# Selective-scan network on one core: GpSimd forms the scan inputs of layer 0 two states at a time

## The reference, cut to what matters

```python
dts, Bsx, Csx = jnp.split(x_dbl, [R, R + N], axis=2)
delta = jax.nn.softplus(dts + dt_projs_bias[None, :, :, None])
A = -jnp.exp(A_logs).reshape(K, DI, N)
def step(h, inp):
    ul, dl, bl, cl = inp
    dA = jnp.exp(dl[..., None] * A)
    h = dA * h + (dl * ul)[..., None] * bl[:, :, None, :]
    y = jnp.einsum('bkdn,bkn->bkd', h, cl)
    return (h, y)
```

## Time and profile before

| | |
|---|---|
| median of 3 runs | 18,193.1 us (18,173.5 to 18,209.19) |
| profiled execution | 18,181.2 us, its span 18,179.3 us |
| VectorE busy | 15,465.9 us, 85% |
| GpSimd busy | 14,606.0 us, 80% |
| TensorE busy | 13,277.9 us, 73% |
| ScalarE busy | 9,704.7 us, 53% |
| DMA | 2348 MB, mean 129 GB/s |

### The profile page before, as it was taken

The page is one execution under the profiler, slowest core; times in us unless marked ns, Lnnn a source line. Parts: engine busy times, 40 slices in busy tenths (PEclk is TensorE's granted clock), DMA queues, the critical chain, the costliest instruction groups (busy, mean ns, idle before and its releaser), DMA issues.

```text
span 18179.3 us, 131102 instructions
## 1 busy us (share of the span) xinstructions
PE 13277.9 (73%) x29696; PEld 5276.7 (29%) x29696; DVE 15465.9 (85%) x9374; ACT 9704.7 (53%) x9235; POOL 14606.0 (80%) x6213
## 2 busy tenths in 40 slices
PE   6776767767677686776767767677676776777767
PEld 2222322223222232222322223222232222322223
DVE  8888878888888888888888888888888888888888
ACT  4445744457444574445744456444564445644456
POOL 7996779967789677996778967799677996779967
PEclk9998989989899898998989989899898998989989
DMA  4442244422444224442244422444224442244422
GB/s 153 165 166 87 74 152 165 166 88 74 153 165 166 87 74 154 166 166 86 74 156 163 166 88 74 155 163 166 87 74 155 164 166 87 74 155 163 166 86 74
DMA packets 662527, 2348.03 MB, mean 129 GB/s; under 512 B 75452, under 2 KB 97224, under 8 KB 661704
## 3 DMA queue, kind: packets, MB, share of 16 engines
q1 hardware_dynamic: 661704, 2339.01, 37.3%
HBM read 2322.98 MB, written 15.73 MB: 129 GB/s over the span
## 4 chain that ended last, share of the span: by engine, by line
POOL 29%; PE 25%; issue 23%; DVE 12%; DMA 5%; ACT 4%; POOLq 1%; DVEq 0%; SPq 0%; ACTq 0%
POOL room L829 20%; PE bank L474 11%; DMA room<-bc_rows 5%; DVE room L1087 4%; PE bank L354 4%; PE bank L483 3%; POOL room L838 3%; PE bank L398 2%; DVE room L1107 2%; PE bank L508 2%; DVE room L1008 2%; PE bank L426 2%; POOL room L787 2%; POOL room L812 1%; DVE room L1016 1%
## 5 line engine op out<-in xcount | busy, mean ns | idle before, releaser
L1008 DVE TENSOR_TENSOR_SCAN room<-bank,room 128x1024 f32<-128x1024 f32 x3072 | 6964.6, 2279 | 530.9 <-ACT bank L613 428.1
L829 POOL TENSOR_TENSOR room<-room 128x1024 f32<-128x1024 f32 x3072 | 7177.0, 2364 | 190.9 <-DMA room<-bc_rows 128.2
L426 PE MATMUL bank<-room,identity 128*128 128x512 f32 x12288 | 6367.3, 646 | 267.3 <-DVE y L1027 252.6
L613 ACT ACTIVATE bank<-room,a 128x1024 f32<-128x1024 f32 x3072 | 3401.6, 1115 | 4910.0 <-DVE room L1008 4906.4
L474 PE MATMUL bank<-room,identity 128*128 128x512 f32 x6144 | 3135.3, 658 | 1231.9 <-DVE room L1107 908.2
L1087 DVE TENSOR_TENSOR_SCAN room<-bank,room 128x1024 f32<-128x1024 f32 x1536 | 3438.9, 2273 | 19.9 <-POOL room L884 4.0
L1016 DVE TENSOR_TENSOR room<-room,bank 128x1024 f32<-128x1024 f32 x2544 | 3044.3, 1197 | 368.7 <-PE bank L413 367.1
L426 PEld LDWEIGHTS bank<-room,identity 128*128 128x128 f32 x12288 | 2468.7, 204 | 2892.1 <-issue 2187.1
L413 PE MATMUL bank<-parts,pick_row 96*128 96x512 bf16 x5088 | 1602.9, 397 | 2333.7 <-DVE room L1016 2264.0
L884 POOL TENSOR_TENSOR room<-room 128x1024 f32<-128x1024 f32 x768 | 2330.9, 3058 | 63.2 <-POOL room L876 63.2
L474 PEld LDWEIGHTS bank<-room,identity 128*128 128x128 f32 x6144 | 1257.2, 210 | 3048.8 <-issue 2672.9
(11 more groups left out here) (98 smaller groups left out, 11593.6 us busy)
## 6 DMA issues: line engine op xcount, KB each, us to landing
room<-bc_rows SPq DMA_DIRECT2D x4368, 512.0 KB, 4.3
wx<-in_w_x SPq DMA_DIRECT2D x65, 162.0 KB
bc_rows<-xdbl SPq DMA_DIRECT2D x72, 128.0 KB, 2.0
xT<-in_x SPq DMA_DIRECT2D x8, 768.0 KB, 5.6
out_x<-xT SPq DMA_DIRECT2D x8, 768.0 KB, 4.4
win<-in_w_in SPq DMA_DIRECT2D x16, 288.0 KB, 3.2
room<-in_w_in SPq DMA_DIRECT2D x16, 288.0 KB, 4.0
room<-in_w_out SPq DMA_DIRECT2D x16, 288.0 KB, 4.3
```

What stands on the lines that cost most here:

```text
L426: ins = nc.tensor.matmul(bank[:, YACC + h, :], identity[:, :], state0[:, g % STATES, halves(h)], start=(n == 0), stop=(n == N - 1))
L613: nc.scalar.activation(whole(DECAY0[g % 2]), delta0[:, j, :], ACT.Exp, scale=a0[:, col:col + 1]).then_inc(S["decay"], note("decay", (i, j, ...
L829: nc.gpsimd.tensor_tensor(source0[:, g % SOURCES, :], du0[:, j, :], b_ring0[:, g % BROWS, :], ALU.mult).then_inc(S["source"], note("source ...
L1008: nc.vector.tensor_tensor_scan(run(state0[:, g % STATES, :]), run(whole(DECAY0[g % 2])), run(source0[:, g % SOURCES, :]), 0.0, ALU.mult, A ...
```

## The change

Two neighbouring units, n even and n + 1, share one instruction on GpSimd and one DMA on SyncE. The source instruction reads `du0[j]` twice (a broadcast over the pair), two neighbouring slots of the B ring, and writes two neighbouring slots of `source0`. It adds 2 to the semaphore `source`, and the scans of both units wait for that. SyncE fills two slots with one DMA of 1 MB, once the pair of sources two pairs before is made. SOURCES goes from 5 to 6 and STATES from 8 to 7, in the same memory. The rows of C, all other operations and their places in GpSimd's list by unit stay as they are.

```diff
--- before.py
+++ after.py
@@ -25,7 +25,9 @@
 
 UNITS = [(i, j, n) for i in range(K) for j in range(J) for n in range(N)]
 PASSES = K * J
-SOURCES, STATES, BROWS, CROWS = 5, 8, 4, 3
+SOURCES, STATES, BROWS, CROWS = 6, 7, 4, 3
+
+PAIR = 2
 
 POOL_LAG, SUM_LAG = 3, 4
 
@@ -149,7 +151,7 @@
 
 
         delta0, du0 = room[:, 0:3, :], room[:, 3:6, :]
-        source0, state0 = room[:, 9:14, :], room[:, 14:22, :]
+        source0, state0 = room[:, 9:15, :], room[:, 15:22, :]
         b_ring0, c_ring0 = room[:, 29:33, :], room[:, 33:36, :]
 
         delta1 = room[:, 0:3, :]
@@ -187,7 +189,7 @@
         HSUM, DECAY_ROWS, DECAY_COLS = 2, 4, 6
 
         names = ["load_wx0", "load_wx1", "load_win1", "load_wz0", "load_wz1", "load_wout0", "load_wout1",
-                 "bc_stored", "b_row0", "b_row1", "b_row2", "b_row3", "c_row0", "c_row1", "c_row2",
+                 "bc_stored", "b_pair0", "b_pair1", "c_row0", "c_row1", "c_row2",
                  "b_line0", "b_line1", "b_line2", "c_line0", "c_line1",
                  "xz", "silu", "mm", "ev", "stat", "gs", "xn", "pad", "conv", "u",
                  "p1", "r1", "p2", "parts", "parts_pool", "ex", "w1", "ln", "wm", "corr", "raw", "dl", "corr_pool", "raw_pool", "dl_pool", "du",
@@ -274,9 +276,13 @@
                     if (j, n) == (0, 0):
                         sp.wait_ge(S["bc_stored"], at("bc_stored", (0, i), b))
                         sp.sem_inc(rows_open, 1)
-                    if g >= BROWS:
-                        sp.wait_ge(S["source"], at("source", UNITS[g - BROWS], b))
-                    spread_row(b_ring0[:, g % BROWS, :], i % 2, n, f"b_row{g % BROWS}", (i, j, n))
+                    if g % PAIR == 0:
+                        if g >= BROWS:
+                            sp.wait_ge(S["source"], at("source", UNITS[g - BROWS], b))
+                        kind = f"b_pair{g // PAIR % PAIR}"
+                        sp.dma_start(b_ring0[:, g % BROWS:g % BROWS + PAIR, :],
+                                     bc_rows[i % 2, n:n + PAIR, :].unsqueeze(0).broadcast_to([P, PAIR, T])).then_inc(
+                            S[kind], note(kind, (i, j, n), 16))
                     if by_pool(i, j, n):
                         c = POOLED.index((i, j, n))
                         if c >= CROWS:
@@ -823,11 +829,13 @@
                 if n == 0:
                     pool.wait_ge(S["du"], at("du", (0, i, j), b))
                 if g >= SOURCES:
-                    pool.wait_ge(S["scan"], at("scan", UNITS[g - SOURCES], b))
-                kind = f"b_row{g % BROWS}"
+                    pool.wait_ge(S["scan"], at("scan", UNITS[g - SOURCES + 1], b))
+                kind = f"b_pair{g // PAIR % PAIR}"
                 pool.wait_ge(S[kind], at(kind, (i, j, n), b))
-                nc.gpsimd.tensor_tensor(source0[:, g % SOURCES, :], du0[:, j, :], b_ring0[:, g % BROWS, :],
-                                        ALU.mult).then_inc(S["source"], note("source", (i, j, n)))
+                nc.gpsimd.tensor_tensor(source0[:, g % SOURCES:g % SOURCES + PAIR, :],
+                                        du0[:, j:j + 1, :].broadcast_to([P, PAIR, T]),
+                                        b_ring0[:, g % BROWS:g % BROWS + PAIR, :],
+                                        ALU.mult).then_inc(S["source"], note("source", (i, j, n), PAIR))
 
             def weigh(b, g):
                 i, j, n = UNITS[g]
@@ -843,7 +851,8 @@
                 du(b, 0, 0, 0)
                 du(b, 0, 0, 1)
                 for g in range(len(UNITS)):
-                    source(b, g)
+                    if g % PAIR == 0:
+                        source(b, g)
                     i, j, n = UNITS[g]
                     if g >= POOL_LAG and by_pool(*UNITS[g - POOL_LAG]):
                         weigh(b, g - POOL_LAG)
@@ -1002,7 +1011,7 @@
                     return ap[:, ::-1] if back else ap
 
                 dve.wait_ge(S["decay"], at("decay", (i, j, n), b))
-                dve.wait_ge(S["source"], at("source", (i, j, n), b))
+                dve.wait_ge(S["source"], at("source", (i, j, n - n % PAIR), b))
                 if g >= STATES:
                     dve.wait_ge(S["sum"], at("sum", UNITS[g - STATES], b))
                 nc.vector.tensor_tensor_scan(run(state0[:, g % STATES, :]), run(whole(DECAY0[g % 2])),
```

## The result

The changed kernel takes 18,227.97 us (median of 11 runs, 18,212.85 to 18,249.42); the kernel before, on the same chip, 18,173.5 us (18,149.54 to 18,209.19). The ratio is 1.0031, 95% interval [1.0022, 1.004]: slower by 0.3%, where 0.2% faster was forecast. The profiled spans, 18,226.8 against 18,179.3 us, differ by 47.5 us. The forecast time, its range (18,115 to 18,215) and its sign are all wrong.

A forecast was written before the change was run, and what follows sets the result against it. GpSimd's lateness at second-tile ends was taken as the stretch to follow, VectorE's waits being mostly for ScalarE's decay. 8 x (6.8 - 2.05) = 38 us less gave 18,143 profiled, forecast 18,155 us, 0.2% faster; range 18,115 to 18,215.

The forecast's parts named there:

- The pair, 4.5 us: On GpSimd, one 2048-column source instruction takes 4.5 us, against 4.66 us for two of 1024 columns.
- Its rows, 5.3 us to landing: A pair's 1 MB DMA of rows of B lands 5.3 us after issue, under a cover of 6.8 us.
- GpSimd's 128 us of waits for them nearly gone: Sign to look for: GpSimd's 128 us of waits for the pairs' row DMAs nearly vanish.
- The ends of the second tiles, -6.8 us an image: GpSimd's new order starts the next tile's first scan earlier after seven second tiles, 6.8 us an image in sum.
- the walks: Step-by-step timelines of the seven second tiles; gains of 0.65, 1.15, 0.70, 0.56, 1.29, 1.35 and 1.11 us.
- The start, +2.05: Each image's scan 0 waits for the whole first pair, so VectorE starts 2.05 us later.
- Eight state slots to seven, nothing: Scan g waits for the sum of g - 7; TensorE's sums come in time, so costed at nothing.
- the first scan aside, a scan finds both halves of a pair ready: On VectorE, only an image's first scan pays for waiting on a whole pair; others wait no longer.
- gained 0.65 at scan 0': Direction 0, end of second tile: the next tile's first scan starts at 202.0 instead of 202.65.
- The rivals: Nothing moves (18,190 us, chance 0.22); second half of the pair becomes the wait (0.11); more than counted (17,990, 0.05).
- The slower one: After second tiles, scan 0' waits for both halves of its pair, 2.2 us more; up to 18,333 us; chance 0.11.
- the 100 named as a sign of error: If VectorE's waits for sources pass 100 us, the forecast is wrong.

The follow-up runs named there:

- the moved wait mended: Changed kernel with even scans waiting for a source count one lower (18,197.77 us, ratio 1.0022), or with the source wait written before the decay wait (18,204.27 us, 1.0019).
- the shared count: Changed kernel, but even scans wait for a source count one lower, the same number as their decay count; 18,197.77 us, ratio 1.0022.
- GpSimd's order alone: Kernel before, with GpSimd making sources two at a time but each row of B still on its own DMA; 18,356.47 us, ratio 1.01.

## Why the prediction was wrong

- **The pair, 4.5 us:** right, 4.53. **Its rows, 5.3 us to landing:** 4.7. "GpSimd's 128 us of waits for them nearly gone": 33.6. The 6.15 us of the Trainium skill ("DMA: Bandwidth & Descriptors", section Bandwidth, for a load issued from GpSimd), weighed against it, would have put the landing too late; the 4.7, of a load issued from SyncE, include the way from the issue.
- **The ends of the second tiles, -6.8 us an image:** right in sum, -6.4, though the seven lie closer (0.66 to 1.09) than the walks said (0.56 to 1.35). That the sum fits so well is in part luck: with the moved wait mended the ends give 7.5 to 7.8, so a gain larger than forecast met a loss that was not in the forecast.
- **The start, +2.05:** right, +2.08.
- **Eight state slots to seven, nothing:** right, 0.9999.
- **"the first scan aside, a scan finds both halves of a pair ready", at no cost in the wait itself:** the step that failed. It looked at when the source is there, not at how the wait is coded. A count that differs from the decay's puts the decay's wait on a register instruction, +0.156 us at each of the 25 scans an image whose decay comes last, by count 3.9 us an image. Taking it away won 3.7 or 2.8 us an image of layer 0 in the traces and 21 us between runs on one chip: 20 to 30 us of the 47.5.
- **Missing: direction 7** (+2.8 us an image, put at nothing). The sum costed the sources only by their own length, not by what VectorE does beside them: 2.2 us of a held operation, and in the first tile 1.8 more behind it, with TensorE at its low level. Splitting that one pair won 1.5 us an image alone, 3.2 with the shared count.
- **Missing: the third tile** (+3.2, put at nothing). "gained 0.65 at scan 0'" was taken as won for good. 3.2 us an image (up to 6.4 in other kernels) come back before scan 2 of the third tile, in front of `collect`, whose idle time grew from 495.6 to 523.5 us. All kernels that gain at the ends show it (the one that loses there, with GpSimd's order alone, has +1.9). TensorE's clock goes with it: in directions 4 to 6 of the 13 traces this stretch takes 9.6 us where full speed was granted throughout (82 times), 11.3 where the level was 0.50 for a part of it (94), and 11.3 to 12.6, mostly 12.3, where it was 0.50 for twice as long (136; the clock read from scan 0' up to `collect`). In directions 0 to 2 it is 10.6 us in every image of the changed kernel, while the kernel before took 8.9 in 10 of 24. Why some kernels are at the low level more often here than others, and whether holding it off would win the time, no run shows.
- The rivals were wrong as well. The slower one (the second half of the pair) named a real thing, but a small one: 1.5 to 1.7 us an image, not 15.4. The waits for sources rose to 125.6 us, over the 100 named as a sign of error; 8 x 7.0 = 56 of it is the start, as counted, another 56 stands at scans 0' and 13 at scans 14.

Together: the forecast sum was -38 us. The stretches it named came to 8 x (2.1 - 6.4) = -34 us; those it left out came to 8 x (3.2 + 4.0 + 2.8) = +80 us. The 20 to 30 us of the moved wait lie across all of them but the start. The kernel that keeps all of the change but the 2048-column instruction and the second count has a span 44 us under the kernel before, so that instruction, with what hangs on it, is where the forecast and the result part. The rest of the +80, outside direction 7, is not taken apart further: with the wait mended, "third" and "rest" still hold +4.4 us an image.

## What to carry to other kernels

When an edit changes how much an instruction adds to a semaphore, look at which instruction each wait lands on in the program: two waits that shared one count may part, and the wait that ends last must be on the instruction itself. A wider instruction on GpSimd can hold a VectorE operation to its end. Here it held the norm's (4.99 us instead of 2.83), which reads and writes SBUF, while the scans, which read one operand from PSUM, kept their 2.28 us. So list what stands beside it before counting the overhead saved. Here order and paired transfers together were worth 0.14%, and the wide instruction took it away: try them apart before taking both.

## What the runs showed of the hardware

- VectorE started a scan 0.033 us after ScalarE's end when the scan itself held the wait, 0.189 us when a register instruction ahead of it did, with the check of the sum between them (medians of 232 scans in each kernel; 188 to 208 of them stand at it, in the others another wait ended last).
- VectorE's norm operation (96x1024, SBUF to SBUF) ended 0.54 to 0.55 us after the end of the GpSimd operation beside it, whether that was one of 1024 columns (2.83 us for the VectorE one) or of 2048 (4.99). GpSimd's own was drawn out too: 2.79 instead of 2.36, 4.96 instead of 4.53.
- Eight equal matmuls after equal waits took 5.39 or 3.69 us, at a granted clock of 0.70 and 1.00 over the first 3.69 us, and the pattern held for a whole image: 3.4 us an image in a layer that no edit touched.
